# Moving the low halves of the down projection's weights from POOL to DVE in the first pair

## The reference, cut to what matters

```python
x = L0_attn_x                       # (4, 2048, 512)
xn = _layernorm(x, axis=-1)
r, k, v = xr @ Wr.T, xk @ Wk.T, xv @ Wv.T      # xr, xk, xv: xn mixed with xn of the token before
att = (sigmoid(r) * wkv_v4(k, v, wkv_w, wkv_u)) @ Wo.T
hidden = fwht(silu(xn @ W1.T) * (xn @ W3.T))   # 2048 wide
x = x + att + hidden @ W2.T
```

## The kernel before, in words

| step | 0 | 1 | 2 | 3 | 4 | 5 | 6 | 7 | 8 | 9 | 10 | 11 | 12 | 13 | 14 | 15 | turn |
|---|---|---|---|---|---|---|---|---|---|---|---|---|---|---|---|---|---|
| split | 0 | 1 | 2 | 3 | 4 | 5 | 6, 7 | 8 | 9 | 10, 11 | 12 | 13, 14 | 15 | 16 | 17 | 18 | 19 |
| used behind piece 2 | | 0 | 1 | 2 | 3 | 4 | 6 | 7 | 8 | 10 | 11 | 13 | 14 | 15 | 16 | 17 | |
| used behind the pieces | | | | | | 5 | | | 9 | | 12 | | | | | | 18, 19 |

## Time and profile before

### The profile page before, as it was taken

The page is one execution under the profiler, slowest core; times in us unless marked ns, Lnnn a source line. Parts: engine busy times, 40 slices in busy tenths (PEclk is TensorE's granted clock), DMA queues, the critical chain, the costliest instruction groups (busy, mean ns, idle before and its releaser), DMA issues.

```text
span 2724.8 us, 33882 instructions
## 1 busy us (share of the span) xinstructions
PE 2665.6 (98%) x11616; PEld 2181.7 (80%) x11616; DVE 2205.9 (81%) x2962; ACT 1318.0 (48%) x2115; POOL 243.0 (9%) x180
## 2 busy tenths in 40 slices
PE   7998999999999999999999999999999999999999
PEld 5676778888888888888888888888888888888887
DVE  6798987888878888688886888878888788878775
ACT  6655556444544445444464444644455444554442
POOL 3297820000000000000000000000000000000000
PEclk9999999999999999999999999999999999999999
DMA  6787687787878778687787877878687787876777
GB/s 237 279 309 246 239 284 251 251 263 232 273 240 274 241 244 283 226 276 241 250 280 230 269 235 263 271 238 272 220 276 251 250 264 228 272 244 222 226 233 266
DMA packets 244951, 691.50 MB, mean 254 GB/s; under 512 B 31920, under 2 KB 31920, under 8 KB 244272
## 3 DMA queue, kind: packets, MB, share of 16 engines
q1 hardware_dynamic: 244784, 689.34, 76.2%
HBM read 575.94 MB, written 113.30 MB: 253 GB/s over the span
## 4 chain that ended last, share of the span: by engine, by line
PE 87%; DVE 8%; ACT 2%; issue 2%; DMA 1%; POOL 1%; SPq 0%; ACTq 0%; DVEq 0%
PE gamma L863 12%; PE gamma L865 12%; PE gamma L866 12%; PE acc L873 10%; PE acc L875 10%; PE acc L874 10%; PE gamma L945 4%; PE gamma L947 4%; PE gamma L946 4%; PE alpha L866 2%; PE alpha L865 2%; PE alpha L863 2%; PE alpha L946 1%; PE alpha L947 1%; PE alpha L945 1%
## 5 line engine op out<-in xcount | busy, mean ns | idle before, releaser
L1059 ACT ACTIVATE step<-gamma 128x512 f32<-128x512 f32 x512 | 305.7, 597 | 840.9 <-PE gamma L866 817.9
L863 PE MATMUL gamma<-xs_high,wring 128*128 128x512 f32 x1280 | 500.2, 391 | 14.2 <-DVE step L1514 8.3
L865 PE MATMUL gamma<-xs_high,wring 128*128 128x512 f32 x1280 | 498.9, 390 | 0.0
L866 PE MATMUL gamma<-xs_low,wring 128*128 128x512 f32 x1280 | 498.8, 390 | 0.0
L873 PE MATMUL acc<-vring,hid 128*128 128x512 f32 x1232 | 481.5, 391 | 14.2 <-POOL vring L744 6.7
L875 PE MATMUL acc<-vring,hid 128*128 128x512 f32 x1232 | 479.9, 390 | 0.0
L874 PE MATMUL acc<-vring,hid 128*128 128x512 f32 x1232 | 479.9, 390 | 0.0
L863 PEld LDWEIGHTS gamma<-xs_high,wring 128*128 128x128 f32 x1280 | 240.9, 188 | 69.3 <-issue 11.2
L873 PEld LDWEIGHTS acc<-vring,hid 128*128 128x128 f32 x1232 | 231.3, 188 | 68.9 <-issue 14.8
L866 PEld LDWEIGHTS gamma<-xs_low,wring 128*128 128x128 f32 x1280 | 240.8, 188 | 50.2
L865 PEld LDWEIGHTS gamma<-xs_high,wring 128*128 128x128 f32 x1280 | 240.9, 188 | 49.8
(11 more groups left out here) (171 smaller groups left out, 4779.8 us busy)
## 6 DMA issues: line engine op xcount, KB each, us to landing
wring<-u_split SPq DMA_DIRECT2D x336, 512.0 KB, 4.2
vring<-d_split SPq DMA_DIRECT2D x288, 512.0 KB, 4.3
wring<-r_split SPq DMA_DIRECT2D x168, 512.0 KB, 4.2
raw<-spilled SPq DMA_DIRECT2D x160, 256.0 KB, 4.2
spilled<-step SPq DMA_DIRECT2D x128, 256.0 KB, 4.3
wlast<-u_split SPq DMA_DIRECT2D x112, 256.0 KB, 3.3
u_split<-wring SPq DMA_DIRECT2D x48, 512.0 KB, 3.3
res<-x SPq DMA_DIRECT2D x16, 1024.0 KB, 8.0
```

Of the source, the lines that this page charges most:

```text
L863: pe.matmul(bank[:, :], w[:, 0, col], high, start=fresh and kt == 0, stop=False, skip_group_check=True)
L865: pe.matmul(bank[:, :], w[:, 1, col], high, start=False, stop=False, skip_group_check=True)
L866: last = pe.matmul(bank[:, :], w[:, 0, col], low, start=False, stop=kt == 1, skip_group_check=True)
L1059: act.activation(to, bank[:, :], ACT.Copy).then_inc(u_copied, 1)
```

## The change

The 20 subtractions that form the low halves of the down units leave POOL's list, and 20 of the same shape enter DVE's, in the first pair's up steps right behind `hidden_b(s, j - 1)` and ahead of the step's second recurrence slot; unit 19 follows `hidden_a(s, 15)` in the turn. They count on a semaphore of their own, `down_lo`; `split_lo` now counts POOL's units alone. PE, SP and POOL wait for whichever of the two belongs to the unit. Operands, ACT's work and the DMAs stay as they were.

```diff
--- before.py
+++ after.py
@@ -75,6 +75,7 @@
 
 SPLITS = first_splits()
 SPLIT_AT = {u: n for n, u in enumerate(SPLITS)}
+POOL_LOW_AT = {u: n for n, u in enumerate(u for u in SPLITS if u[0] != "d")}
 RAWS = first_raws()
 RAW_AT = {u: n for n, u in enumerate(RAWS)}
 RAW = 8
@@ -91,7 +92,7 @@
 
 def freed_by(raw):
 
-    return SPLIT_AT[("u", raw[1], 0) if raw[0] == "w1" else ("u", raw[1], 3) if raw[0] == "w3" else raw]
+    return ("u", raw[1], 0) if raw[0] == "w1" else ("u", raw[1], 3) if raw[0] == "w3" else raw
 
 
 WK = 12
@@ -263,7 +264,7 @@
         ha_hi, hb_hi = counted("ha_hi", ND), counted("hb_hi", ND)
         wkv_exp = counted("wkv_exp", 32)
 
-        split_lo = sem("split_lo")
+        split_lo, down_lo = sem("split_lo"), sem("down_lo")
         sum_made = sem("sum_made")
         rstd_ready = counted("rstd_ready", 2)
 
@@ -346,6 +347,10 @@
                 return last_stored, 16 * (unit[1] + 1)
             return w_stored[unit[2]], 16 * (unit[1] + 2)
 
+        def low_made(unit):
+
+            return (down_lo, unit[1] + 1) if unit[0] == "d" else (split_lo, POOL_LOW_AT[unit] + 1)
+
         def previous_in_place(unit):
 
             if unit[0] == "r":
@@ -497,7 +502,8 @@
             def load_residual(s, h):
 
                 if is_first(s) and h == 0:
-                    sp.wait_ge(split_lo, max(freed_by(RAWS[m]) for m in range(len(RAWS)) if RAW_SLOT[m] >= 4) + 1)
+                    for unit in {RAW_SLOT[m]: freed_by(RAWS[m]) for m in range(len(RAWS)) if RAW_SLOT[m] >= 4}.values():
+                        sp.wait_ge(*low_made(unit))
                 if h:
                     wait(sp, out_stored, s, 16)
                 else:
@@ -609,7 +615,7 @@
                 else:
                     source = w_units[name[0]][name[1]]
                 if held_before(m) is not None:
-                    sp.wait_ge(split_lo, freed_by(held_before(m)) + 1)
+                    sp.wait_ge(*low_made(freed_by(held_before(m))))
                 slot = RAW_SLOT[m]
                 sp.dma_start(raw[slot][:, :], source).then_inc(raw_loaded[slot], 16)
 
@@ -618,13 +624,13 @@
             def store_split(unit):
 
                 n = SPLIT_AT[unit]
-                sp.wait_ge(split_lo, n + 1)
+                sp.wait_ge(*low_made(unit))
                 to = r_from(unit[1]) if unit[0] == "r" else d_from(DOWN_A[unit[1]]) if unit[0] == "d" \
                     else u_from(unit[1], unit[2])
                 sp.dma_start(to, split_place(unit).bitcast(f32)).then_inc(stored_in(unit)[0], 16)
                 if unit[0] == "r":
                     return
-                while raws[0] < len(RAWS) and freed_by(held_before(raws[0])) <= n:
+                while raws[0] < len(RAWS) and SPLIT_AT[freed_by(held_before(raws[0]))] <= n:
                     load_raw(raws[0])
                     raws[0] += 1
 
@@ -753,7 +759,7 @@
                 if j == 0:
                     pool.wait_ge(w2_psum, 2 * FT)
                 else:
-                    pool.wait_ge(split_lo, SPLIT_AT["u", j - 1, 2] + 1)
+                    pool.wait_ge(split_lo, POOL_LOW_AT["u", j - 1, 2] + 1)
                 pool.tensor_tensor(sums[:, 1, :], w3[:, near], w3[:, far], ALU.add).then_inc(sum_made, 1)
                 pool.tensor_tensor(sums[:, 2, :], w1[:, near], w3[:, near], ALU.subtract).then_inc(sum_made, 1)
                 pool.wait_ge(sum_made, 4 * j + 1)
@@ -771,8 +777,6 @@
             for i in range(3):
                 lo(("u", 0, i))
             for j in range(FT):
-                for i in down_splits(j):
-                    lo(("d", i))
                 lo(("u", j, 3))
                 if j + 1 < FT:
                     make_sums(j + 1)
@@ -780,8 +784,6 @@
                         lo(("u", j + 1, i))
                 if j in (5, 9):
                     inverse_root(1, (j - 5) // 4)
-            for i in down_splits(FT):
-                lo(("d", i))
             with pool.Fori(2, PAIRS) as r:
                 inverse_root(r, 0)
                 inverse_root(r, 1)
@@ -789,7 +791,7 @@
         @block.tensor
         def _(pe):
             def wait_split(unit):
-                pe.wait_ge(split_lo, SPLIT_AT[unit] + 1)
+                pe.wait_ge(*low_made(unit))
 
             def up_weights(s, j, i):
 
@@ -1539,6 +1541,14 @@
                 dve.tensor_tensor(u_two[j % 2], u_two[j % 2], gamma[(j + 2) % 3][:, :], ALU.add)\
                     .then_inc(gate_b_sum, 1)
 
+            def down_weights_lo(j):
+
+                for i in down_splits(j):
+                    dve.wait_ge(split_hi, SPLIT_AT["d", i] + 1)
+                    to = split_place(("d", i))
+                    dve.tensor_tensor(to[:, 1, :], split_source(("d", i)), to[:, 0, :].bitcast(f32), ALU.subtract)\
+                        .then_inc(down_lo, 1)
+
             def recurrence(s, j, slot):
 
                 at = FIRST_UP_WKV if is_first(s) else UP_WKV
@@ -1568,6 +1578,8 @@
                 if j:
                     gate_b_applied(s, j - 1)
                     hidden_b(s, j - 1)
+                if is_first(s):
+                    down_weights_lo(j)
                 recurrence(s, j, 1)
                 if j:
                     hidden_a_lo(s, DOWN_A.index(("w2", j - 1)))
@@ -1589,6 +1601,8 @@
                 if not last:
                     mix_item(s + 1, 0)
                 hidden_a(s, FT - 1)
+                if is_first(s):
+                    down_weights_lo(FT)
                 gate_b_applied(s, FT - 1)
                 if not last:
                     mix_rest(s + 1, 0)
```

## The result

| | before | after |
|---|---|---|
| median (range, executions) | 2727.08 us (2725.44 to 2729.17, 5) | 2741.93 us (2738.43 to 2742.40, 5) |
| ratio, with its 95% interval | | 1.0047 (1.0037 to 1.0058) |
| profiled execution: time, span | 2726.61, 2724.8 us | 2742.09, 2740.3 us |
| PE, DVE, ACT, POOL busy, share of the span | 98%, 81%, 48%, 9% | 97%, 81%, 48%, 8% |
| mean granted clock of PE | 0.997 | 0.993 |

The account below looks back on a forecast made before the run. The prediction took DVE's list to set the pace in the first pair's later up steps (97.1 of 99 us busy). Its terms, 2.0 + 3.0 + 4.5 + 0.5 = +10.0 us, gave 2736.5 us, range 2726 to 2746.

Parts of the forecast that it names:

- The sign and the mechanism: First pair's up phase: slower by 10.0 us, mainly because PE waits for DVE's low halves in steps 6, 9 and 11.
- faster: Rival: shared memory path or POOL is the real bound; -8 us, 2719 us; chance 0.10.
- its own deciding point: The faster rival decides once DVE's relief passes some 1.5 us for each of 11 units, or the three waits are hidden.
- No change: Rival: PE's late restarts are hidden, only step 6 and about 2 us left; 2729 us, up to 2732; chance 0.20.
- Twice as slow: Rival: each added DVE instruction waits like L1537, 12.7 us beside the three steps' 9.5 us; 2749 us; chance 0.14.
- DVE's load against POOL's relief (+0.5 us): Eleven units where DVE is full: 0.60 us added, 0.5 us given back each, 1.1 us rounded down to 0.5.
- Two of the signs: Changed profile's up phase: POOL's busy time falls by 25 to 30 us, DVE's rises by some 2 to 5 us.
- the reading of rows 2: DVE's only long idle time is 8.2 us in two places before L1519, at step 0 and step 9 (4.8 us).
- Steps 6, 9 and 11 (2.0 + 3.0 + 4.5 us): PE waits longer for units 6, 10 and 13, going on 2.6, 2.9 and 7.6 us later; loss +2.0, +3.0, +4.5 us.
- the forecast's own clock: Step 11: reciprocal starts at 296.57, PE goes on at 303.1, 7.6 us later than before; wait 8 to 10 us.
- The clock: PE's matmuls behind long waits start 0.43 us apart at 1.2 GHz; step 9 gets 0.7 us for that.
- Counted at nothing: Shorter PE waits for up-projection weights (11.0 us) and later raw loads: nothing counted, up to 3 us if a load is late.

Follow-up runs that it names:

- changed, once more: The changed kernel as it is, run again beside later experiments on the same chip: 2740.18 us, ratio 1.0039, +14.3 us against the kernel before.
- 17 units on DVE: Changed kernel, but POOL forms the low halves of down units 6, 10 and 13 as before, DVE the other 17: 2730.55 us, ratio 1.0011.
- units 6, 10, 13 on DVE: Kernel before, but DVE forms the low halves of down units 6, 10 and 13 at the change's place, POOL the other 17: 2734.54 us, ratio 1.0024.
- the same, early: DVE forms only units 6, 10 and 13, directly behind hidden_a, ahead of the reciprocal; POOL forms the other 17: 2725.80 us, ratio 0.9997.
- DVE's load alone: Kernel before plus 20 DVE subtractions of 128x400 on a tile nobody reads, at the change's places; POOL's work kept: 2738.21 us, ratio 1.0043.
- POOL's relief alone: Kernel before with the 20 down units' low halves left out; units count as ready with their high half: 2714.38 us, ratio 0.9955.
- early in steps 6, 9, 11: Changed kernel, but in steps 6, 9 and 11 DVE forms the low halves directly behind hidden_a, ahead of the reciprocal: 2729.53 us, ratio 1.0007.
- early in step 11: Changed kernel, with DVE's low halves directly behind hidden_a, ahead of the reciprocal, in step 11 alone: 2738.38 us, ratio 1.0041.
- early in steps 6, 9: Changed kernel, with DVE's low halves directly behind hidden_a in steps 6 and 9 alone: 2732.14 us, ratio 1.0021.
- PE's order, kernel before: Kernel before, but in steps 6, 9 and 11 PE takes the down unit's first two tiles only behind piece 3: 2727.90 us, ratio 0.9999.
- PE's order, changed kernel: Changed kernel, but in steps 6, 9 and 11 PE takes the down unit's first two tiles only behind piece 3: 2734.56 us, ratio 1.0021.
- PE's order, 17 units on DVE: PE takes those tiles behind piece 3 in steps 6, 9, 11; POOL forms units 6, 10, 13, DVE the other 17: 2731.50 us, ratio 1.0011.

## Why the prediction was right in its direction, and where its terms were off

To see where the first pair loses its time I take DVE's instruction that forms block a's sum (L1519 before, L1521 in the changed kernel) as a milestone of each step, and its start in a kernel's profile less its start in the profile of before. This is how much that difference grows, in us, between step 0, step 5, step 13 and step 0 of the next pair (at 133, 200, 326 and 495 us before):

| kernel | step 0 to 5 | step 5 to 13 | to the next pair | sum |
|---|---|---|---|---|
| changed | 3.5 | 7.7 | 2.2 | 13.4 |
| changed, once more | 2.9 | 9.5 | 2.9 | 15.3 |
| 17 units on DVE | 2.5 | -3.7 | 3.4 | 2.1 |
| units 6, 10, 13 on DVE | 0.0 | 6.6 | 2.0 | 8.6 |
| the same, early | 0.0 | -1.4 | 1.6 | 0.1 |
| DVE's load alone | 3.7 | 4.0 | 2.8 | 10.6 |
| POOL's relief alone | -1.8 | -9.4 | -0.5 | -11.7 |
| early in steps 6, 9, 11 | 1.2 | -2.1 | 2.8 | 1.9 |
| early in step 11 | 3.3 | 2.6 | 4.0 | 9.8 |
| early in steps 6, 9 | 3.2 | 2.3 | 4.0 | 9.5 |
| PE's order, kernel before | 0.0 | -0.7 | 3.3 | 2.6 |
| PE's order, changed kernel | 2.6 | -0.5 | 7.0 | 9.0 |
| PE's order, 17 units on DVE | 2.5 | -1.4 | 5.7 | 6.8 |

Each row is one execution. The third column is uncertain by some 3 us: PE's order in the kernel before has 3.3 us there, though its median is that of the kernel before; all rows but that of POOL's relief lie at 1.6 us or more, so the profile of before may itself be short there. The first column is uncertain by up to 2 us (two kernels with the same instructions up to step 5 have 1.2 and 3.3).

**The sign and the mechanism hold.** PE waits for L1549 in exactly the three steps named, DVE idles behind it at L1498, and the early place, which changes nothing but where DVE stands with these units, takes the loss from +14.9 and +14.3 us to +1.2. In the table the three waits are the difference between 7.7 or 9.5 and -2.1 us, 9.8 to 11.6 us; by the medians they are 13.1 to 13.7 us, by the ratios 8.7 to 10.9; 9.5 had been put. Of the rivals, "faster" fell at its own deciding point: it needed 1.5 us of relief for each of 11 units, 16.5 us, and 13.3 us was there for all 20. "No change" needed the late restarts to be hidden, and DVE's 11.9 us of idle time before L1498 says that they weren't. "Twice as slow" needed DVE's load to be paid in full, and with POOL's relief it is not.

**DVE's load against POOL's relief (+0.5 us): right in the sum, by luck, and not in its parts.** An added instruction was put at 0.60 us and took 1.05. But DVE's other two-operand instructions got shorter by nearly as much, and DVE's busy time rose by 1.1 us. Into the sum went 11 × 0.60 = 6.6 us of load and 11 × 0.5 = 5.5 us of relief. Measured alone they were 10.5 us, with 400 columns in place of 512, and 13.3 us: both terms were too small, and the errors cancel. Only the relief over all 20, put at 10 us, came near. All 20 on DVE at the early place cost +1.2 us, the 17 +2.9; 0.5 is inside the interval of the first and at the lower end of that of the second (0.5 to 5.5 us). The two sides fall at different places, which the prediction didn't see: the 17 units cost 2.5 us up to step 5 and give back 3.7 by step 13, where POOL's relief is worth most (9.4 of 11.7 us).

The Trainium skill's "SBUF — State Buffer", section on SBUF's two separate sides, calls the port pair of DVE and GpSimd an exclusive lock; the shortened neighbours agree with it (L1539 at 1070 ns in place of 1225). Its consequence, a gain because DVE holds the pair for less time than POOL did, was not seen: load and relief together came to +1.2 us.

**Two of the signs came out otherwise.** POOL's busy time fell by 36 us and not by 25 to 30: the 20 instructions had 29.8 us, and those that stayed got shorter too. DVE's rose by 1.1 us where 2 to 5 had been put. And DVE had a third long idle time before, of 3.1 us at step 0 (at 136.89 us, in front of L1496 for another tile), which the reading of rows 2 left out; nothing hangs on it.

**Steps 6, 9 and 11 (2.0 + 3.0 + 4.5 us): near in the sum, off in the split by the medians, not by the trace.** In the table step 11's early place is worth 5.1 to 6.9 us beside the waits of steps 6 and 9 and 4.4 without them; that of steps 6 and 9 is worth 5.4 to 7.2 and 4.7. The medians divide it otherwise, 1.8 and 5.0 us for step 11, 8.1 and 11.3 for steps 6 and 9; five executions of the changed kernel and five of the one early in step 11 can't settle which, and the latter loses 4.0 us in the third column, which varies by itself.

Step 11 went by the forecast's own clock: PE goes on 310.44 - 304.00 = 6.44 us behind the reciprocal's start, 303.1 - 296.57 = 6.53 had been put. Only the length of the wait was wrong, 6.42 us and not 8 to 10. PE came to it at the reciprocal's start (304.0 us), where before it came 2.9 us ahead of it (293.7 against 296.57). That PE is held up in steps 6 and 9 explains a third of this: with the early place in those two steps it came 0.9 us ahead and waited 6.96 us. The rest isn't explained. L1498 starts 12.7 us behind the reciprocal's start, put at 11.4 (7.6 before); that is about what the lower clock takes there (matmuls 0.43 us apart from 311.00 to 313.13 us, 0.23 us from 313.48 us on: 1.0 us).

Step 6 is where a step failed: "L1528 ahead of it had stood behind the vring instructions, and with them gone I take 1.1 us off". The instruction before was

```profile
214.98 1.75 DVE L1528 SCALAR_TENSOR_TENSOR step<-step 128x512 f32<-128x512 f32 x1 [0.55 <-ACT step L1064]
```

It did get shorter (L1530 took 0.80 us), but it now waited 1.18 us for ACT's tanh in place of 0.55. Against L1521, which started at 218.87 us (before: L1519 at 213.75), L1535 ends at 3.8 us, where it ended at 4.1 before: 0.3 us were gained, not 1.1. Then the two low halves took 2.34 us, 1.2 each, in place of 0.6 to 1.2. PE went on 5.1 us behind L1521, put at 4.0, so the wait became 7.72 us.

**The clock was counted too low.** Behind 7.72 us of idle time PE's matmuls started 0.43 us apart for eight intervals (224.51 to 227.92 us), then 0.23 us; behind the 4.43 us of step 9 it was the same up to 279.02 us:

```profile
278.59 0.63 PE L867 MATMUL gamma<-xs_high,wring 128*128 128x512 f32 x1
279.02 0.50 PE L868 MATMUL gamma<-xs_low,wring 128*128 128x512 f32 x1
...
279.59 0.40 PE L867 MATMUL gamma<-xs_high,wring 128*128 128x512 f32 x1
279.82 0.39 PE L868 MATMUL gamma<-xs_low,wring 128*128 128x512 f32 x1
```

In step 9 L1498 starts 7.3 us behind PE's restart (281.46 and 274.19 us), where 4.9 had been put. Only 0.7 us had been put for this in step 9 and as much in step 11, nothing of its own in step 6. The granted clock fell to 0.94 over the up phase (0.98 before) and to 0.93 between 264 and 363 us, where it had been 1.00. PE's idle time grew from 20.0 us of 230 to 30.0 us of 243. The other 3 us are matmuls that ran slower: PE was busy for 213.0 us in place of 210.0, with three matmuls fewer. Against the early place the changed kernel has 3.6 us of them (204.7 and 201.1 us busy for the same 852 matmuls, in the table of stretches above), so some 4 of the 12 to 14 us between these two kernels are the clock.

**Counted at nothing.** The late raw load came: ACT waited 5.6 us for it once, in step 15. PE stood still for 1.3 us behind it (until 368.75 us), and DVE for none, as its reciprocal ran until 368.2 us. The kernel with the early place has the same wait (5.5 us) and costs +1.2 us in all. The waits for up-projection weights did shrink (wlast from 3.1 to 1.7 us, those of wring gone); what that bought wasn't measured by itself.

**What stays open.** The 17 units and the three give 2.9 + 6.8 = 9.7 us apart and 14.3 or 14.9 together (by the ratios 9.5 against 10.6 and 12.8, each uncertain by 3 us or so). In the table the excess lies between steps 5 and 13: -3.7 + 6.6 = 2.9 against 7.7 and 9.5. One reading is that DVE, idle behind L1498 there, can't collect what POOL's relief gives back; it was argued from the table and not tried by itself. Nor is it settled why PE's order gives back only some half of the loss: up to step 13 its profile is 2.0 us longer than that of before (the early place's 0.9 us shorter), and it loses 7.0 us more between step 13 and the next pair.

## What to carry to other kernels

An operation moved to another engine pays for its place in that engine's list, and not only for its length: twenty moved here cost 15 us at one place, and 1 us with six of them a few instructions ahead. Before such a move, look for the units that the consumer wants soonest, follow what they will stand behind (a wait for a third engine, a long reciprocal), and put those first. Where DVE sets the pace, removing a wait of PE can give nothing, and taking work off POOL can give more than the waits for that work.

## What the runs showed of the hardware

POOL's float32 work slows DVE's two-operand SBUF instructions (L1537 took 1225 ns beside a busy POOL and 677 ns beside an idle one) so much that leaving out 20 POOL instructions was worth 13.3 us, twice the 6.7 us that PE waited for them; DVE's busy time fell by 11.2 us with them. And waits of PE for a down unit of 3.7 to 7.9 us were followed by matmuls at the lower of the clock's levels (1.2 of 2.4 GHz): the length of a wait isn't all that it costs.
